# Fetching the last of 56 columns by plain row transfers instead of an indirect gather

## What is computed

```
# first network (one pass over the edges); tab0 rows: z, v@Wg, two scalars
z = x @ Wa;  z_src = z[src];  z_dst = z[dst]
e = leaky_relu([w * z_src, z_dst] @ att_w)
alpha = softmax of e over the edges of each dst
h = segment_sum(alpha * z_src, dst)
gate = sigmoid([x, segment_max(w * x[src] @ Wg), segment_mean(w * x[src])] @ gate_w)
x = layernorm(x + gate * h)
# second network: 3 layers (three passes over the edges); tabkv rows: k | v
edge = relu(ln(edge_attr) @ eW1 + eb1) @ eW2 + eb2
for l in range(3):
    h = ln(x);  q = (h @ Wq)[dst];  k, v = (h @ Wkn)[src], (h @ Wvn)[src]
    alpha = softmax over dst of q . (k + edge @ Wke) / sqrt(8), 8 heads
    agg = segment_sum(alpha * (v + edge @ Wve), dst)
    x = x + gated(agg, h) @ Wout;  x = x + mlp(ln(x))
x = layernorm(x1 + ln(x))
```

## Time and profile before

| | |
|---|---|
| runs | 9159.48 us median (9159.09 to 9161.79) |
| profiled execution | 9160.98 us, its span 9159.2 us |
| busy, share of the span | GpSimd 70%, VectorE 63%, PE 40%, ScalarE 31% |
| granted TensorE clock, mean | 0.686 of full speed |
| gathers of the layers, L546 | 4704 |
| gathers of the first pass, L546 | 1568 |
| SP's issues of srcI | 112 |

### The profile page before, as it was taken

One profiled execution on the slowest core, in us unless ns is written; L12 is line 12 of the kernel. 1 busy time (PEld: TensorE's weight loads), 2 busy tenths in 40 slices (PEclk: granted clock), 3 DMA queues, 4 the chain that ended last, 5 costly groups with the idle time before them and its releaser, 6 DMA issues.

```text
span 9159.2 us, 45368 instructions
## 1 busy us (share of the span) xinstructions
PE 3667.0 (40%) x9857; PEld 2190.5 (24%) x9857; DVE 5799.7 (63%) x6114; ACT 2862.4 (31%) x2181; POOL 6365.8 (70%) x6734
## 2 busy tenths in 40 slices
PE   2677777776323233223342232322242222223325
PEld 1333333333122122212121221222222122212212
DVE  1666666666366776676437667767744776677673
ACT  0566666666122222222222222222221222222223
POOL 6677777774577777777457777777736777777762
PEclk9988888888656566555666665665576656656557
DMA  3455555554433443444234334434314443444331
GB/s 52 161 192 180 186 179 174 175 184 148 132 131 131 139 149 131 139 140 141 64 108 148 132 132 141 147 131 139 125 49 138 139 149 131 137 141 141 131 110 48
DMA packets 405487, 1247.08 MB, mean 136 GB/s; under 512 B 196101, under 2 KB 253910, under 8 KB 360006
## 3 DMA queue, kind: packets, MB, share of 16 engines
q0 software_dynamic: 215104, 429.19, 17.4%
q1 hardware_dynamic: 169606, 468.24, 14.6%
q10 hardware_dynamic: 20736, 349.23, 9.5%
HBM read 808.34 MB, written 437.84 MB: 136 GB/s over the span
## 4 chain that ended last, share of the span: by engine, by line
POOL 52%; issue 20%; PE 17%; ACT 7%; DVE 2%; DMA 1%; DVEq 1%; ACTq 0%; POOLq 0%; SPq 0%
POOL G L546 49%; PE PS L696 7%; PE PS L689 6%; ACT S L910 4%; POOL qexp L599 1%; PE PS L777 1%; POOL QQ L588 1%; PE PS L781 1%; ACT hid L886 1%; PE PS L666 1%; POOL s2exp L565 1%; POOL S L552 1%; POOL G L588 1%; ACT S L851 0%; ACT L855 0%
## 5 line engine op out<-in xcount | busy, mean ns | idle before, releaser
L546 POOL DMA_INDIRECT G<-tabkv,srcI x4704 | 4438.4, 944 | 1433.6 <-issue 1433.6
L756 PE MATMUL PS<-Wkvp,EA 128*128 128x256 f32 x4704 | 1672.9, 531 | 4296.3 <-DVE PX L1438 4217.8
L756 PEld LDWEIGHTS PS<-Wkvp,EA 128*128 128x128 f32 x4704 | 1253.4, 274 | 4716.5 <-DVE PX L1438 4381.7
L546 POOL DMA_INDIRECT G<-tab,srcI x1568 | 1481.4, 945 | 571.9 <-issue 507.2
L959 ACT ACTIVATE QQ<-QQ 128x3584 f32<-128x3584 f32 x84 | 538.4, 6410 | 3313.5 <-DVE PX L1438 3063.1
L1435 DVE TENSOR_TENSOR PS<-PS,G 128x512 f32<-128x512 f32 x588 | 408.4, 695 | 1593.3 <-DMA G<-tabkv,srcI 1575.3
L973 ACT ACTIVATE S<-SX 128x4480 f32<-128x4480 f32 x81 | 663.7, 8194 | 1238.4 <-DVEq L1462 1238.4
L689 PE MATMUL PS<-xT,W1p 128*128 128x512 f32 x1568 | 768.5, 636 | 252.2 <-ACT xT L847 243.1
L1424 DVE TENSOR_TENSOR_SCAN QQ<-PS,QQ 128x456 f32<-128x456 f32 x672 | 679.4, 1082 | 207.9 <-ACT QQ L959 192.3
L1461 DVE TENSOR_TENSOR_SCAN SX<-PS,SX 128x456 f32<-128x456 f32 x756 | 763.2, 1082 | 12.2
L696 PE MATMUL PS<-hid,W2p 128*128 128x512 f32 x1568 | 710.9, 596 | 34.2 <-ACT hid L886 31.5
(11 more groups left out here) (311 smaller groups left out, 4090.8 us busy)
## 6 DMA issues: line engine op xcount, KB each, us to landing
st<-S ACTq DMA_DIRECT2D x81, 2240.0 KB, 7.8
EA<-eaT SPq DMA_DIRECT2D x84, 1792.0 KB, 7.8
QQ<-qexp SPq DMA_DIRECT2D x84, 1792.0 KB, 7.3
st<-S ACTq DMA_DIRECT2D x27, 3668.0 KB, 12.0
G<-tabkv,srcI POOLq DMA_INDIRECT x4704, 2.5
xe<-in_edge_attr SPq DMA_DIRECT2D x28, 1792.0 KB, 8.1
qexp<-zeros SPq DMA_DIRECT2D x28, 1792.0 KB, 12.6
eaT<-eaC ACTq DMA_DIRECT2D x28, 1792.0 KB
```

Of the source, the lines that this page charges most:

```text
L546: nc.gpsimd.indirect_dma_start(out=G[:, u, t, :], out_offset=None, in_=tab[:, :], in_offset=IND(ap=srcI[:, u, t:t + 1], axis=0)).then_inc( ...
L756: last = mm(PS[:, b + j // 2, 2 * P * (j % 2):2 * P * (j % 2) + 2 * P], EA[:, u, 4 * s + j, :], Wkvp[:, :], start=True, stop=True)
```

## The change

In each chunk GpSimd gathers columns 0 to 54 only (PLAIN = 55). Column 55 is fetched by SP. With the chunk's `srcI`, SP also fetches the 128 row numbers of that column into one partition, `lastI[0, u, :]`. It loads them into registers, 16 at a time, and issues for each of the 128 edges one plain DMA of one row from the table, at an address from the register, to partition p of G0 or G1. In the layers these 128 transfers are cut in four quarters with a semaphore each: three follow the chunk's `EA` fetch, the fourth stands between the next chunk's `QQ` and `EA` fetches. In the first pass they are cut in halves: one after the chunk's inputs, one behind the next chunk's `srcI`, ahead of its xe. VectorE waits for all of a chunk's parts before the step that reads column 55. At a layer's start all four quarters of chunk 0 stand ahead of the wait for the scatter of the queries.

```diff
+QUARTER = P // 4
+ROW_SEM = 16 * QUARTER * (NCH // 2)
+PLAIN = C - 1
+LAST_GOT = 16 * (C - 1 - 8 * (PT - 1))
...
+            def plain_rows0(u, i, halves):
+                hold(sp, waits_sp, last0_in[u], i * 16 + 16)
+                for q in halves:
+                    for p0 in range(q * P // 2, (q + 1) * P // 2, 16):
+                        _, nodes = nc.values_load_multi_w_load_instructions(
+                            lastI[0:1, u, p0:p0 + 16], engines=(mybir.EngineType.SP,), min_val=0, max_val=NT * P - 1,
+                            skip_runtime_bounds_check_because="src holds node numbers below N")
+                        for p, node in enumerate(nodes, p0):
+                            sp.dma_start(G0[p:p + 1, u, PLAIN, :], tab0[bass.ds(node, 1), :]).then_inc(plain0_got[u][q], 16)
-            def loads(c, u, index):
+            def loads(c, u, index, i=0):
                 if index:
                     sp.wait_ge(seen0, c + 1)
                     sp.dma_start(srcI[:, u, :], src_pt[:, bass.ds(c * C, C)]).then_inc(idx0[u], 16)
+                    sp.dma_start(lastI[0:1, u, :], src_pt[:, bass.ds(c * C + PLAIN, 1)].rearrange("p o -> o p"),
+                                 allow_slow_non_contiguous=True).then_inc(last0_in[u], 16)
+                    plain_rows0(1 - u, i - 1 + u, range(1, 2))
...
             for u in range(2):
                 loads(u, u, False)
+            sp.wait_ge(n0_tab, 16 * NG)
+            plain_rows0(0, 0, range(2))
+            plain_rows0(1, 0, range(1))
             with sp.Fori(1, NCH // 2) as i:
                 for u in range(2):
-                    loads(2 * i + u, u, True)
+                    loads(2 * i + u, u, True, i)
+                    plain_rows0(u, i, range(1))
+            plain_rows0(1, NCH // 2 - 1, range(1, 2))
...  layers: sources also fetches lastI; plain_rows is plain_rows0 with G1, tabkv and four quarters
                 table_weights(l + 1)
+                plain_rows(0, 0, range(4))
                 hold(sp, waits_sp, q_put, (l + 1) * (16 * NT))
...
                 for u in range(2):
                     queries(u)
+                plain_rows(1, 0, range(3))
                 with sp.Fori(1, NCH // 2) as i:
                     for u in range(2):
                         sources(2 * i + u, u)
                         queries(2 * i + u)
+                        plain_rows(1 - u, i - 1 + u, range(3, 4))
                         features(2 * i + u, u)
+                        plain_rows(u, i, range(3))
+                plain_rows(1, NCH // 2 - 1, range(3, 4))
...
-                        gathers(u, G1, tabkv, lambda t: got1[u][t // 8], range(C // 2, C))
+                        gathers(u, G1, tabkv, lambda t: got1[u][t // 8], range(C // 2, PLAIN))
...
-                dve.wait_ge(got0[u], i * (16 * C) + 16 * C)
+                dve.wait_ge(got0[u], i * (16 * PLAIN) + 16 * PLAIN)
                 dve.sem_inc(seen0, 1)
+                for q in range(2):
+                    dve.wait_ge(plain0_got[u][q], i * (8 * P) + 8 * P)
...
+                                dve.wait_ge(got1[u][s], l * (NCH // 2 * LAST_GOT) + i * LAST_GOT + LAST_GOT)
                                 dve.sem_inc(seen1, 1)
+                                for q in range(4):
+                                    dve.wait_ge(plain_got[u][q], l * ROW_SEM + i * (16 * QUARTER) + 16 * QUARTER)
```

More of the change, by code:

```diff
@@ L98, in build @@
         srcI = sb("srcI", [P, 2, C], i32)
+        lastI = sb("lastI", [1, 2, P], i32)
         firstI = sb("firstI", [P, 1], i32)
@@ L178, in build @@
         got1 = [[sem(f"got1_{u}_{k}") for k in range(PT)] for u in range(2)]
+        last_in = [sem(f"last_in{u}") for u in range(2)]
+        last0_in = [sem(f"last0_in{u}") for u in range(2)]
+        plain0_got = [[sem(f"plain0_got{u}_{q}") for q in range(2)] for u in range(2)]
+        plain_got = [[sem(f"plain_got{u}_{q}") for q in range(4)] for u in range(2)]
         seen1 = sem("seen1")
@@ L395, in _ @@
                 sp.dma_start(srcI[:, u, :], src_pt[:, u * C:(u + 1) * C]).then_inc(idx0[u], 16)
+                sp.dma_start(lastI[0:1, u, :], src_pt[:, u * C + PLAIN:u * C + C].rearrange("p o -> o p"),
+                             allow_slow_non_contiguous=True).then_inc(last0_in[u], 16)
             edge_weights(0)
@@ L482, in sources, with plain_rows @@
                     sp.dma_start(srcI[:, u, :], src_pt[:, bass.ds(c * C, C)]).then_inc(idx1[u], 16)
+                    sp.dma_start(lastI[0:1, u, :], src_pt[:, bass.ds(c * C + PLAIN, 1)].rearrange("p o -> o p"),
+                                 allow_slow_non_contiguous=True).then_inc(last_in[u], 16)
+                def plain_rows(u, i, quarters):
+                    hold(sp, waits_sp, last_in[u], l * (NCH // 2 * 16) + i * 16 + 16)
+                    for q in quarters:
+                        for p0 in range(q * QUARTER, (q + 1) * QUARTER, 16):
+                            _, nodes = nc.values_load_multi_w_load_instructions(
+                                lastI[0:1, u, p0:p0 + 16], engines=(mybir.EngineType.SP,), min_val=0, max_val=NP - 1,
+                                skip_runtime_bounds_check_because="src holds node numbers below N")
+                            for p, node in enumerate(nodes, p0):
+                                sp.dma_start(G1[p:p + 1, u, PLAIN, :], tabkv[bass.ds(node, 1), :]).then_inc(plain_got[u][q], 16)
                 def queries(c):
@@ L556, in _ @@
             pool.wait_ge(idx0[0], 16)
-            gathers(0, G0, tab0, lambda t: got0[0])
+            gathers(0, G0, tab0, lambda t: got0[0], range(PLAIN))
             pool.wait_ge(p_rp, 16)
@@ L569, in _ @@
             pool.wait_ge(idx0[1], 16)
-            gathers(1, G0, tab0, lambda t: got0[1])
+            gathers(1, G0, tab0, lambda t: got0[1], range(PLAIN))
             with pool.Fori(1, NCH // 2) as i:
@@ L577, in _ @@
                             hold(pool, waits_pool, m_pe, 28 * (2 * i + u - 1) + (4 * k - 3 if k > 1 else 0))
-                        gathers(u, G0, tab0, lambda t: got0[u], range(8 * k, 8 * k + 8))
+                        gathers(u, G0, tab0, lambda t: got0[u], range(8 * k, min(8 * k + 8, PLAIN)))
             def fix_and_fetch(st, R, o, outs, rows):
@@ L1430, in _ @@
                             steps = slice(8 * s, 8 * s + 8)
-                            dve.wait_ge(got1[u][s], l * (NCH // 2 * 128) + i * 128 + 128)
-                            if s == PT - 1:
+                            if s < PT - 1:
+                                dve.wait_ge(got1[u][s], l * (NCH // 2 * 128) + i * 128 + 128)
+                            else:
+                                dve.wait_ge(got1[u][s], l * (NCH // 2 * LAST_GOT) + i * LAST_GOT + LAST_GOT)
                                 dve.sem_inc(seen1, 1)
+                                for q in range(4):
+                                    dve.wait_ge(plain_got[u][q], l * ROW_SEM + i * (16 * QUARTER) + 16 * QUARTER)
                             dve.wait_ge(kv_ready, n * PT + s + 2)
```

## The result

The changed kernel takes 9559.08 us (median of 4 runs, 9557.39 to 9563.97) against 9159.28 for the kernel before on the same chip: a ratio of 1.0437, 95% interval 1.0419 to 1.0455. It is 4.4% slower, 482 us above the forecast of 9077, inside the wide range and on rival 1's side.

What follows compares the result with a forecast made beforehand. GpSimd's gathers were taken to bound the layers, and PE and ScalarE the first pass. Layers -104.9, chunk 0's gather -1.2 and the first pass's start +24 gave -82, so 9077 us; own range 9050 to 9110, wide range 9045 to 10,350.

Steps and rivals of the forecast that it cites:

- rival 1: SP's row transfers become the bound and the kernel is slower, from 0.53 us per row: 9640 or 12,080 us; chance 0.36.
- Does SP keep up?: Step weighing SP's time per chunk against the gathers: layers 59.8 us against 68.7, first pass 61.6 under 72.46.
- r: SP's time per fetched row, covering issue, address and register load: 0.45 us, with bounds of 0.30 and 0.75.
- issue and address: SP's issue of one row transfer with its address instructions: 0.36 us per row, low end 0.30, high end 0.64.
- register loads: SP's loading of row numbers into registers, 16 words a batch: 0.09 us per row, with a floor of 0.
- other transfers: SP's whole-chunk transfers in a layer: three at 0.43 us, 0.65 for lastI, and waits, 2.2 us per chunk.
- rival 2: Single rows share DMA engines and queue, land after the last gather, and VectorE waits: about 9160 us; chance 0.07.
- The 9640: Kernel time in us at 0.56 us per row, from the Trainium skill's 200 ns per register: +480 us.
- rival 3: The first pass gains as well if PE's holds on GpSimd move up: 35 us more saved, 9042 us; chance 0.04.
- The sign that it named: In the slower case VectorE's wait names the rows' DMA rather than the gathers.
- The start of a layer: Chunk 0's four quarters delay QQ by 37 us, VectorE ends chunk 0 some 5 us later: cost 0.
- The shift at the first pass's start: Chunk 0's and 1's rows delay the first pass's start, and the pass keeps its shift: +24 us.

## Why the prediction was wrong

The step that failed is "Does SP keep up?". Its structure was right: 128r plus a few transfers against the gathers' 68.7, with the sign decided at r near 0.52. Its sizes were not. SP's time per chunk of a layer, in us; the measured terms are worked out from the trace over 20 chunks:

| term | forecast | measured |
|---|---|---|
| issue and address, 128 rows | 46.1 (0.36 each) | 52.7 (0.412) |
| register loads | 11.5 (0.09) | 9.7 (0.077 and a gap) |
| other transfers | 2.2 | 1.8 |
| slow rows' excess | none | 3.7 |
| longer pauses | none | 2.3 |
| rest | | 1.6 |
| sum | 59.8 | 71.8 |

- **Issue and address.** The value was built from the spacing of two whole-tile issues with 0.25 put in for 0.33, on the ground that the address was in their gap. The issue was well sized (0.228); the address was not. In the gap of 0.10 us before ewC, the trace of before has one register instruction (MOVE, 29 ns). A row whose number was loaded needs two of its own (37 and 29 ns), and its gap is 0.184; with a fixed address rows start 9.66/32 = 0.30 apart, though their issue is then the longer (0.252). This is +6.6 us.
- **Slow rows.** The forecast had no term for them; its one word on the matter was "DMA is 41% busy", against rival 2. A mean share says nothing of the microseconds after a store of 2.24 MB, and the run with that store cut to one column shows that these cost 3.5 us a chunk. With 66 us of undisturbed work and 2.3 of pauses SP would just keep up with 68.7; this is what tipped the layers from a gain to a loss.
- **Pauses.** Gaps of 2.4 to 2.6 us at the branch of SP's loop, once in two chunks, and of 0.35 us on the way, 2.3 us per chunk. The new loop body comes from memory, 3.96 MB in 484 packets of the instruction queue against 0.25 MB in 31. That it is the fetching which makes SP pause is likely and was not tested.
- **Register loads.** Nearly right (0.077 against 0.09 a row). The Trainium skill, "Runtime: NRT & Kernel Launch" (Instruction fetch mechanics), puts them at about 200 ns a register even in bulk; from SBUF this case shows 56 ns a word and 335 a load, so the measurement decides against it here. The 9640 that the page's figure gave was nearer to the result than the forecast, but through a term that turned out small.

**The first pass** was the larger mistake: 61.6 us a chunk forecast, 82.4 measured, and 293 of the 400 us. The same row price applies (52.7), the loads take 12.1, the slow rows' excess 10.7, pauses 2.6, other transfers 2.7, and 1.6 is left over. In its middle SP had 11 us of reserve by the forecast, and the disturbed rows alone eat that: per chunk this pass has two stores of ScalarE's (1.79 and 3.67 MB), a fetch and a store of 1.8 MB of SP's own, where the layers have one store and two fetches. And there was never a gain to set against the risk, since the gathers did not bound it; that step held (rival 3 is out: with the rows cheap the pass stays at 72.55).

**Rival 1** was the case that came true, through r: counted as the forecast counted it, (71.8 - 2.2)/128 = 0.54 in the layers and (82.4 - 4)/128 = 0.61 in the first pass. The sign that it named, VectorE's wait on the rows' own DMA, came too. Its price for r = 0.56, +4.0 a layer chunk and +3.2 a first-pass chunk, was taken with one r for both stages; the split was +1.9 and +9.9, with the first pass the dearer. **Rival 2** didn't come in the form given: SP sends the rows late; it isn't their landing, since with a fourth of the same rows on the second queue the layers run at the gathers' pace.

**What held:** x4620 gathers at 944 ns; 104.9 us as the worth of 84 gathers, which two kernels whose SP keeps up confirm (their layer chunk is 68.7); and no gain from the first pass's gathers. The start of a layer also costs next to nothing, though for another reason than given: the forecast has VectorE end chunk 0 some 5 us later, and by SP's third srcI it is 38 later (148.3 us after the layer's first srcI, 110.5 before), since SP issues that srcI only behind chunk 1's 96 rows. GpSimd's third chunk starts on time even so (177.4 us after the first srcI, 178.9 before). The shift at the first pass's start came out larger than forecast: the first start of ScalarE's score step, L910 before and L958 now, is 357.5, with about 348 forecast and 324.7 before, so 33 us for 23. Even with loads and addresses left out the rows delay the first pass's end a little (9.4 us at layer 0's first srcI).

**What stays open:** the nature of SP's pauses, how a store holds up the rows of another queue, and in the first pass the share of each neighbour in the slow rows. There 227 of the 278 slow rows have a store of ScalarE's as the last large transfer ahead of them, but no run took these stores away.

## What to carry to other kernels

Work that is handed to a sequencer needs a budget as an engine has one: per item the issue, each register instruction with its gap and the load, and on top of it what the item waits when a large store drains; here 59.8 of 68.7 us by the forecast were 66 by the undisturbed prices and 71.8 with stalls and pauses. A lead of the relieved engine can hide the shortfall for a while: each layer's first ten chunks ran as forecast. Put such work only where the engine that it relieves bounds: in the first pass there was nothing to win. And when one queue is too short, a share on a second idle one turns a loss of 1.2% into a gain of 1.2%.

## What the hardware showed unexpectedly

- A one-row transfer of 512 or so bytes keeps the issuing queue for 0.228 us (0.252 with a fixed address); from start to start it is 0.30 with a fixed address and 0.412 with one from a loaded register.
- A load of 8, 16 or 32 words from SBUF into registers takes 0.782, 1.229 or 2.118 us.
- While a store of 2.24 MB from another queue drains, four or five single-row issues last about 0.9 us each, and one up to 11 us where three large transfers meet; in the layers it goes away with the store. The issuing engine stands still meanwhile, with whatever is behind it. Behind a fetch of 1.79 MB on SP's own queue the rows keep their pace, at a DMA share of 0.91.
- Two engines that issue such rows side by side keep their pace (0.226 us for SP, 0.234 for ScalarE).
